# A fused LayerNorm, state-space mixer and two-expert MLP kernel: spaced token scatters, deeper output buffers, earlier low parts and a read-out in four array strips

## The reference

```python
xn = layernorm(x)
# mixer
u = xn @ W_x.T + b_x;  g = sigmoid(xn @ W_g.T + b_g)            # 256 channels
h = conv1d(u, conv_w, 3 taps, per channel) + conv_b
u = u * g + h * (1 - g)
dt = clip(mean over all tokens of softplus(xn @ W_dt.T + b_dt), .001, 2)
A_d = exp(-softplus(A_raw) * dt);  B_d = (A_d - 1) / (A + 1e-6) * B_ssm
s_t = A_d * s_(t-1) + B_d * u_t;  y_t = sum over 16 states of C * s_t
mix = layernorm(xn + y @ W_out.T + b_out, ln_g, ln_b)
# experts: token -> experts h and h+1 (mod 8), h from its first two channels
ffn = mean over both of (relu(xn @ W1[e] + b1[e]) @ W2[e] + b2[e])
out = xn + mix + ffn
```

## Time and profile before

| | us |
|---|---|
| runs | 496.3, 497.9, 500.8 (median 497.9) |
| the profiled execution | 493.2 |
| its span | 491.4 |
| granted clock, mean | 0.971 |
| busy PE / weight load / DVE / ACT / POOL | 419.6 / 366.8 / 383.1 / 318.5 / 241.5 |

### The profile page before, as it was taken

The page is one execution under the profiler, slowest core; times in us unless marked ns, Lnnn a source line. Parts: engine busy times, 40 slices in busy tenths (PEclk is TensorE's granted clock), DMA queues, the critical chain, the costliest instruction groups (busy, mean ns, idle before and its releaser), DMA issues. The chain is left out here.

```text
span 491.4 us, 11835 instructions
## 1 busy us (share of the span) xinstructions
PE 419.6 (85%) x3379; PEld 366.8 (75%) x3379; DVE 383.1 (78%) x669; ACT 318.5 (65%) x899; POOL 241.5 (49%) x272
## 2 busy tenths in 40 slices
PE   1158799995379999999999999999998889898990
PEld 1136678874279999999999999999996444476870
DVE  6997667766049999999999998999962347674997
ACT  2697799995157777777665567665645445525982
POOL 4683656667723222343363244643323656676770
PEclk9999999999579999999999999999999999999996
DMA  9997335413111212122232235432213618179454
GB/s 236 267 413 234 93 102 150 124 55 125 52 29 38 43 41 43 32 43 44 43 85 48 43 84 129 101 71 44 43 32 95 157 45 215 44 187 243 130 160 133
DMA packets 111416, 52.77 MB, mean 107 GB/s; under 512 B 48881, under 2 KB 106393, under 8 KB 111385
## 3 DMA queue, kind: packets, MB, share of 16 engines
q1 hardware_dynamic: 106328, 43.48, 33.8%
q0 software_dynamic: 4096, 8.40, 5.8%
q10 hardware_dynamic: 960, 0.52, 0.4%
HBM read 28.12 MB, written 24.25 MB: 107 GB/s over the span
## 5 line engine op out<-in xcount | busy, mean ns | idle before, releaser
L1466 PE MATMUL PS<-AR 128*128 128x128 f32 x1184 | 141.8, 278 | 15.9 <-ACT AR L765 10.7
L1466 PEld LDWEIGHTS PS<-AR 128*128 128x128 f32 x1184 | 137.8, 194 | 17.1 <-issue 10.3
L765 ACT ACTIVATE AR<-PS,VC 128x256 f32<-128x256 f32 x296 | 112.3, 489 | 22.2 <-remote 18.4
L1452 PE MATMUL PS<-XT,RR 128*128 128x256 f32 x296 | 86.3, 292 | 1.4 <-POOL XT L583 1.0
L1453 PE MATMUL PS<-XT,RR 128*128 128x256 f32 x296 | 83.0, 281 | 0.0
L1454 PE MATMUL PS<-XT,RR 128*128 128x256 f32 x296 | 82.8, 280 | 0.0
L577 POOL DMA_INDIRECT sorted_tokens<-RA,posi x64 | 62.8, 981 | 38.2 <-issue 25.0
L583 POOL TENSOR_TENSOR XT<-XTF,XT 128x256 fp32r<-128x256 f32 x35 | 31.8, 908 | 84.4 <-ACT XT L742 84.4
L606 POOL TENSOR_TENSOR AR<-AR,b2p 128x256 f32 x37 | 36.1, 975 | 65.0 <-ACT AR L778 62.5
L778 ACT ACTIVATE AR<-PS 128x128 f32 x74 | 16.5, 275 | 68.3 <-PE PS L1466 61.4
L1452 PEld LDWEIGHTS PS<-XT,RR 128*128 128x128 f32 x296 | 56.2, 190 | 2.4 <-POOL XT L583 1.9
(11 more groups left out here) (236 smaller groups left out, 837.3 us busy)
## 6 DMA issues: line engine op xcount, KB each, us to landing
sorted_tokens<-AR SPq DMA_DIRECT2D x10, 512.0 KB, 5.6
XSIN<-sorted_tokens SPq DMA_DIRECT2D x160, 32.0 KB
sorted_outputs<-AR SPq DMA_DIRECT2D x37, 128.0 KB, 1.9
RA<-in_L_attn_x_dram SPq DMA_DIRECT2D x8, 512.0 KB, 8.1
normalised_tokens<-RA SPq DMA_DIRECT2D x16, 256.0 KB
RB<-normalised_tokens SPq DMA_DIRECT2D x8, 512.0 KB
AR<-in_L_ffn_W_dram SPq DMA_DIRECT2D x15, 256.0 KB, 5.0
out_dram<-RB SPq DMA_DIRECT2D x7, 512.0 KB
```

The source lines that it names most:

```text
L765: nc.scalar.activation(HID[n][:, k, :], ps[2 * n + k // 2][:, (k % 2) * FT:(k % 2 + 1) * FT], ACT.Relu, bias=B1C[:, e, k:k + 1]).then_inc( ...
L1452: T.matmul(bank, W1h[slot][:, w], XT[:, 0:FT], start=True, stop=False)
L1466: ins = T.matmul(ps[5 + h][:, 0:D], HID[n][:, k, h * P:(h + 1) * P], W2S[slot][:, k, :], start=(n == 0 and k == 0), stop=(n == 1 and k == ...
```

## The change

Seven edits. (1) **Scatters.** Block t now waits for projection group 15t/8+3, and each of the last 17 blocks, which have no group to wait for, is preceded by two one-column memsets on POOL. (2) **Low parts and gate pieces.** `NLOW` goes from 3 to 6; DVE makes the low parts of tiles 1 to 5 at fixed spots inside the first four gate pieces (`LOW_AT`), transposes tiles 3 to 6 at others (`TILES_AT`), and the first four state transposes move behind the fourth piece, with the wait for all scatters. (3) **Output slots.** `YSB` has four slots, `AR` grows by one chunk for it; a tile is stored when the one two later has been added. (4) **Read-out.** The 32-row strips of a duo's second pair are in reverse order (`strip`), and each pair's read-out is four matmuls of 32 rows by 64 columns instead of two of 64 by 128; `READ` and `AP2` are filled to suit, by twice as many operations of half the size. (5) `decay` runs two duos ahead instead of one. (6) Groups 12 and 13 leave `VG` (ACT scales them, DVE gains them), and DVE adds the x of group 7 before gain and base of group 6. (7) The dt weights' parts lie in `XT`, so `RR` is one chunk smaller; ACT makes them by three copies instead of two, POOL by two subtractions instead of one, and ACT's first write to `XT` waits for the dt sums.

```diff
-                    c, part = divmod(min(2 * t + 3, 6 * (NCH - 1) - 1), 6)
-                    pool.wait_ge(s_pr[part // 2][part % 2], c + 1)
+                    group = 15 * t // 8 + 3
+                    if group < 6 * (NCH - 1):
+                        c, part = divmod(group, 6)
+                        pool.wait_ge(s_pr[part // 2][part % 2], c + 1)
+                    else:
+                        for n in range(2):
+                            nc.gpsimd.memset(rest[:, t % NREST, n:n + 1], 0.0).then_inc(s_rest, 1)
                     nc.gpsimd.indirect_dma_start(out=xs_dram, in_=XN[:, t, :], in_offset=None,
...
-                return (14 * j + 102) // 29
+                return (14 * j + 88) // 29
+            LOW_AT = {(0, 1): 1, (1, 0): 2, (1, 4): 3, (2, 4): 4, (3, 4): 5}
+            TILES_AT = {(0, 2): 4, (1, 2): 5, (2, 2): 6, (3, 1): 7}
+            NLATE = 4
...
+                    between(piece, 4)
+                    if piece == NLATE - 1:
                         dve.wait_ge(s_ready, NT)
...
+                        for m in range(NLATE):
+                            to_states(0, m)
...
-                    sp.wait_ge(s_yst, i * 16 + 32)
...
+                sp.wait_ge(s_yst, i * 16 + 16 * (NY4 - LATE))
...
-                    for w in range(2):
-                        rows = slice(64 * w, 64 * w + 64)
-                        ins = T.matmul(out_bank(r, w), READ[rows, r, :], SX[q % 2][rows, k * BC:(k + 1) * BC],
-                                       start=False, stop=True)
+                    for ab in range(2):
+                        for w in range(2):
+                            rows = strip(k, w, ab)
+                            cols = slice(64 * ab, 64 * ab + 64)
+                            ins = T.matmul(out_bank(r, w)[cols, :], READ[rows, r, cols], SX[q % 2][rows, k * BC:(k + 1) * BC],
+                                           start=False, stop=True)
...
-                if r % 2 == 0 and 1 <= r // 2 < NDUO - 1:
-                    decay(r // 2 + 1)
+                if r % 2 == 0 and r // 2 + 2 < NDUO:
+                    decay(r // 2 + 2)
...
-        VG = (1, 3, 11, 12, 13, 15)
+        VG = (1, 3, 11, 15)
...
-            scale_gain(12)
-            scale_gain(13)
+            add_x(7)
+            gain(6)
             add_base(6)
-            add_x(7)
             scale_batch(6)
```

More of the change, by code:

```diff
@@ L54, in ssm_moe_layer @@
     NYP = 8
-    NLOW = 3
+    NLOW = 6
     with ExitStack() as ctx:
@@ L174, in scaled @@
             return g + 1 - by_v, by_v
+        NREST = 20
+        rest = sb("rest", [P, NREST, 2])
         wmean = sb("wmean", [P, HB + 1])
@@ L477, in _ @@
                     load_tile(i + 3)
-                    sp.wait_ge(s_yad, i + 1)
-                    sp.sem_inc(s_step2, 1)
-                    sp.wait_ge(s_yst, i * 16 + 32)
-                    sp.sem_inc(s_step2, 1)
-                    sp.dma_start(ys_v[bass.ds(i, 1)].rearrange("o p h d -> p (o h) d"), tile_of(YSB, i)).then_inc(s_yst, 16)
+                    with sp.If(i >= LATE):
+                        store_tile(i)
+            for n in range(LATE):
+                store_tile(bounds[E] + n)
             def load_x(n):
@@ L777, in _ @@
                     for h in range(FH):
[L778 removed]
+                        ins = nc.scalar.activation(YSB[:, bass.ds((i & (NY4 - 1)) * FT + h * D, D)], ps[5 + h][:, 0:D], ACT.Copy, scale=0.5)
                     ins.then_inc(s_ysb, 1)
@@ L1058, in ahead, with between, to_states @@
             def ahead(j):
-                return (14 * j + 102) // 29
+                return (14 * j + 88) // 29
+            LOW_AT = {(0, 1): 1, (1, 0): 2, (1, 4): 3, (2, 4): 4, (3, 4): 5}
+            TILES_AT = {(0, 2): 4, (1, 2): 5, (2, 2): 6, (3, 1): 7}
+            NLATE = 4
+            assert sorted(LOW_AT.values()) == list(range(1, NLOW))
+            def between(piece, spot):
+                if (piece, spot) in LOW_AT:
+                    low_tile(LOW_AT[piece, spot])
+                if (piece, spot) in TILES_AT:
+                    tiles_to(TILES_AT[piece, spot])
+            def to_states(hb, n):
+                w = GB * NC
+                link(V.transpose(UT[hb][:, :, n * w:(n + 1) * w].rearrange("p g c -> p c g"),
+                                 RC[:, hb, gate_cols(n)].rearrange("p (c i) -> p c i", i=Q)))
             for hb in range(HB):
@@ L1089, in _ @@
                         dve.wait_ge(s_xt[1], NCH // 2)
-                    w = GB * NC
-                    link(V.transpose(UT[hb][:, :, n * w:(n + 1) * w].rearrange("p g c -> p c g"),
-                                     z.rearrange("p (c i) -> p c i", i=Q)))
-                    tiles_to(ahead(third + 3))
+                        for m in range(NLATE):
+                            to_states(0, m)
+                            if m == 1:
+                                tiles_to(8)
+                    if piece >= NLATE:
+                        tiles_to(ahead(third + 2))
+                        to_states(hb, n)
+                        tiles_to(ahead(third + 3))
             for hb in range(HB):
```

106 lines of the change are left out of this document (65 added, 41 removed).

## The result

The changed kernel takes 503.6 us (median of 19 runs) against 497.8 us (19 runs) for the kernel before: ratio 1.0125, 95% interval 1.0103 to 1.0147. The forecast was 481 us, a gain.

A forecast was written before the change was run, and what follows sets the result against it. PE bounds the tiles, after a start held up by late PE counts during POOL's indirect transfers. Expert stage -14.5 and state space -2 on the profiled 493.2 give 476.7; the median lies 4.7 higher: 481 us, range 471 to 497.

The forecast's parts named there:

- The step that failed: Last scatters on POOL: memsets would widen their distance from 1.26 to about 1.5 to 1.6 us, a pause after each.
- the whole -14.5 us of the expert stage: Expert stage: tile 36 would start at 351.7 instead of 366.18 us, with late relus gone and low parts earlier.
- Rival B: Scatters: pauses too short, PE's counts arrive when scatters end, at 136 to 138 us; total 496 us, chance 0.18.
- the steeper pacing: Scatters: three blocks more may go directly, giving back 3 to 4 us of what the pauses cost.
- edit 7: Before PE is fed: two more small instructions and a copy, between 0 and +0.7 us, taken as 0.
- The read of the hold-up as POOL's doing: Expert and state-space stages: PE's counts are held up, up to 20 us, while POOL issues indirect transfers without a pause.
- Edit 2's table of tiles: Expert stage on PE: tiles 1 to 5 start at 120.9, 130.4, 136.9, 143.4 and 150.1; 16.3 us gained at tile 5.
- Edit 3: Output slots: 0 at steady state; between 0 and +0.7 us on the first gathers, hidden by the first duos; taken as 0.
- Edit 6: Last groups: DVE saves 0.9 us, ACT gets 2.18 us in its waits; between -0.9 and +1.5, taken as 0.
- Edits 4 and 5: State-space read-out and decays: between -9 and 0 us, taken as -2; the stage would last 57 to 59 us.
- C: Rival on the read-out: a pair's four matmuls run only two at a time, 2.26 us a duo; total 501, chance 0.09.
- D: Rival on the read-out: the eight matmuls run one after another, 4.5 us a duo; total 530 us, chance 0.05.

The follow-up runs named there:

- e15: The changed kernel without the memsets before the last scatters, steeper pacing kept: 465.6 us, ratio 0.9986 to the kernel before on the same chip.
- e6: The changed kernel with all seven edits, run on a chip where PE's counts are not late: 464.9 us, ratio 0.9973 to the kernel before.
- e5: The kernel before, run again with no edit for its profile, on a chip where no count was late: 466.6 us, ratio 0.9988.
- e2: The kernel before with edits 3 and 7 alone (four output slots with later stores, dt weights' parts in XT): 467.8 us, ratio 1.0044.
- e7: The kernel before with edits 4 and 5 alone (read-out in four strips, decays two duos ahead): 469.6 us, ratio 1.0051.
- e11: The changed kernel without edit 4 (old read-out, old READ and AP2 fills): 460.9 us, ratio 0.9882 to the kernel before.
- e13: The changed kernel without edits 4 and 6, stores two tiles late kept: 458.7 us, ratio 0.9825 to the kernel before.

## Why the prediction was wrong

**The step that failed** is edit 1's: "with a gap like that between scatters, the distance of two scatters goes from 1.26 to about 1.5 to 1.6 us". It stayed 1.26, since the 0.30 us between two issues was room that the memsets fit into; e15, without them, ends its scatters within 0.4 us of e6. The step added 0.15 us of work to a gap without asking what fills the gap. With it fell the whole -14.5 us of the expert stage. Rival B had the mechanism (the pauses are too short, counts arrive at the scatters' end), but took everything else to stay as before, 496 us; it was 503.6. Whether real pauses would have freed the counts was not tried either.

**The prices that were missing.** The prediction let the steeper pacing only give time back (3 to 4 us) and put edit 7 at 0 to +0.7 us, "two more small instructions and a copy". Neither was asked what it does while counts are late. In the trace 3.7 us are lost in stage 1 to waits behind unbroken runs of scatters, and the last projections then fall into such a run, so that tile 1 goes from 139.8 to 146.8. Edit 7 adds a wait for one of those counts: PE, done with the projections at 117.3, started tile 0 at 122.3. But tile 0 then stood until 140.1 for another count. So the trace gives most of the 7 us to where the runs of scatters lie, in which edit 1's pacing has a part; no run where counts are held up separates the two edits. Edit 7's other price, 0.06 us more on each tile, is in every trace.

**The read of the hold-up as POOL's doing** was too strong. It goes with POOL's issues in the earlier trace rows and in four more waits after (70.65, 99.60, 138.74, 398.07, all released 1.4 to 1.7 us after the end of an unbroken run), but e5 has the same issues and no late count. The issues alone do not do it.

**Edit 2's table of tiles** came out where the counts were prompt, in part by luck: forecast 120.9, 130.4, 136.9, 143.4, 150.1 for tiles 1 to 5; e6 has 116.7, 123.1, 129.5, 136.6, 145.8, from a start 3.7 us earlier than the 113.4 it counted from. Moved by these 3.7 us, the forecast is 3 to 4 us late for tiles 2 to 4, because the load of tile 3 was no wait (SP issued three loads in a row, 112.81 to 124.02), and right for tile 5 only because that one stood 2.4 us for its low part, which was not foreseen. Against e5 the last tile gained 8.0 us.

**Edit 3** was put at 0 to +0.7 us, hidden by the first duos. It moved the first gather from 3.0 to 5.8 us behind the injection. How much of the 2.8 us reaches the end is not settled: in e2 none did, in e6 the lead over e5 shrank by 2.4 us between the last tile and the first gather. From the first gather to the end all runs without the hold-up take 97 to 103 us. That POOL's gathers bound the second half stood in the forecast only as a reason against edit 4's gain, not as the term that edits 3 and 6 would add to. **Edit 6**, put at 0 between -0.9 and +1.5, cost 1.7 to 2.3.

**Edits 4 and 5** gave the stage -3.5 us in e7 (-2 forecast), and all eight matmuls overlap: 0.69 us, where C has 2.26 and D 4.5, so both are out. On the held-up chip the stage did not shrink but grew by 2.2 us; the copy at 398.07 fits the reason that the prediction named last, held-up counts that grow. The Trainium skill's "TensorEngine Tiling (Array Packing)", section "Restrictions and Gotchas", has it that different row tiles cannot use one PSUM bank at once, and "TensorE: Matmul & The Clock Gate", section "Part 3: Packing small matmuls — row/col tiling", that weight loads overlap matmuls in flight only in other row groups; the traces bear out neither for this case: two strips that write one bank (on different partitions), and two pairs that share row strips, run within 0.69 us, where one of the 16 records is 0.37 to 0.43 us. The extra fills were called covered, "uncovered they would cost 2 us"; in e7 they were not covered and took 2.8 us more, in the changed kernel the last tile starts within 1 us with them and without (e6, e11).

**What stays open:** what holds up PE's counts, whether it belongs to a chip or to a session, how much of the loss is edit 1's pacing and how much edit 7's wait, and whether e13 is faster there. That e13 would be better than the changed kernel there is likely, as edit 6's cost shows in that trace too; that it would beat the kernel before is not, as edits 1 and 7 are still in it.

## What to carry to other kernels

An instruction put into a gap makes the gap longer only if nothing else fills it: look whether the distance from start to start can grow. When counts of one engine are seen to arrive late, every new wait for that engine is to be priced at that lateness, however small the instruction behind it. Ask the same of every edit that makes a run of the suspected instructions longer. And ask of each stage which resource runs through it from end to end; here it is 64 gathers, 85 to 90 us of the last 97 to 103 without the hold-up, beside which a faster read-out was worth 0.7 us in e7 and cost time in e6.

## What was not expected of the hardware

The same kernel takes 497.8 us in one place and 466.4 to 467.0 us on four chips, with the same scatters and gathers on POOL. In the first, semaphore counts from PE arrive up to 21 us late while POOL issues indirect transfers, at ACT, DVE and POOL alike, and within 0.8 to 1.7 us of its pause; counts from ACT are not late there (DVE's low part at 120.81, 0.03 us after ACT's write). Between the traces of before and e5, 3.6 us of the difference are there by the dt sums, 11.2 at tile 5, 10.6 at the first gather and 26.5 at the end, so more than half of it arises behind the first gather. The same change was 1.25% slower where counts are late and between 0.5% faster and equal where they are prompt (e6): one verdict does not carry over to the other.
